# Value matmuls of two key tiles issued together in every second step of an attention loop

## The reference

```python
q = layer_norm(x) @ Wq            # 2048 x 1024, 16 heads of 64
k, v = split(context @ Wkv)       # 1601 keys, and one null key ahead
sim = einsum('bhid,bhjd->bhij', q * sqrt_scale, k * sqrt_scale)
attn = softmax(where(mask, sim, -max))
out = einsum('bhij,bhjd->bhid', attn, v)
out = layer_norm(out @ Wout)
x = x + out
x = x + ffn(layer_norm(x))        # 256 -> 1024 -> 1024 -> 256
```

## Time and profile before

| | us |
|---|---|
| time, median of 3 runs | 1582.44 (1582.07 to 1584.61) |
| span of the profiled execution | 1574.0 |
| time that lies around the span (median less span) | 8.4 |
| PE busy | 1513.6 |
| DVE busy | 1032.6 |
| ACT busy | 708.4 |
| POOL busy | 777.9 |

### The profile page before, as it was taken

The page is one execution under the profiler, slowest core; times in us unless marked ns, Lnnn a source line. Parts: engine busy times, 40 slices in busy tenths (PEclk is TensorE's granted clock), DMA queues, the critical chain, the costliest instruction groups (busy, mean ns, idle before and its releaser), DMA issues.

```text
span 1574.0 us, 20245 instructions
## 1 busy us (share of the span) xinstructions
PE 1513.6 (96%) x6068; PEld 845.3 (54%) x6068; DVE 1032.6 (66%) x1272; ACT 708.4 (45%) x1169; POOL 777.9 (49%) x657
## 2 busy tenths in 40 slices
PE   5898999999999999999999999999999998999998
PEld 3554555455545544554455445554554453778777
DVE  7784677577767766776677567757776747544442
ACT  3324444644464446445544554455445534232242
POOL 3005666576656665666566566656665646101100
PEclk9998999999999999999999999999999999999999
DMA  5222100110020002000200020003000501101000
GB/s 160 79 82 68 51 7 7 34 57 8 12 60 26 7 16 77 7 8 14 77 7 8 15 77 7 11 10 84 8 8 21 178 7 61 61 14 53 13 14 14
DMA packets 43586, 60.22 MB, mean 38 GB/s; under 512 B 4049, under 2 KB 31636, under 8 KB 42580
## 3 DMA queue, kind: packets, MB, share of 16 engines
q1 hardware_dynamic: 43476, 58.92, 12.7%
HBM read 26.27 MB, written 17.30 MB: 28 GB/s over the span
## 4 chain that ended last, share of the span: by engine, by line
PE 89%; DVE 5%; issue 2%; ACT 2%; POOL 1%; DMA 0%; DVEq 0%; SPq 0%; ACTq 0%; POOLq 0%
PE ps_o L1244 25%; PE ps_s L1263 17%; PE ps_s L1264 12%; PE ps_side L1182 12%; PE ps_side L1325 10%; PE ps_side L1168 3%; PE ps_s L1286 3%; PE ps_side L1203 2%; PE ps_side L1158 1%; PE ps_side L1159 1%; DVE mxh L925 1%; PE ps_side L1191 1%; PE ps_o L1142 1%; PE ps_o L1144 1%; DVE khl L914 1%
## 5 line engine op out<-in xcount | busy, mean ns | idle before, releaser
L424 POOL TENSOR_TENSOR acc<-acc,prob 128x512 f32<-128x512 f32 x522 | 669.1, 1299 | 338.5 <-ACT prob L777 311.9
L777 ACT ACTIVATE prob<-ps_s,keybias 128x512 f32<-128x512 f32 x832 | 527.5, 685 | 560.7 <-PE ps_s L1264 518.4
L925 DVE TENSOR_REDUCE mxh<-ps_side 128x1 f32<-128x804 f32 x512 | 485.6, 991 | 152.9 <-PE ps_side L1182 150.3
L1244 PE MATMUL ps_o<-prob,vp 128*64 128x512 f32 x1664 | 448.2, 616 | 0.0
L1263 PE MATMUL ps_s<-qdup,khl 128*128 128x512 f32 x832 | 373.0, 448 | 9.2 <-issue 4.6
L1263 PEld LDWEIGHTS ps_s<-qdup,khl 128*128 128x128 f32 x832 | 156.1, 188 | 365.5 <-issue 261.9
L1264 PE MATMUL ps_s<-qrest,krest 128*128 128x512 f32 x832 | 329.5, 396 | 0.0
L1182 PE MATMUL ps_side<-khl,qdup 128*128 128x402 f32 x1024 | 249.3, 360 | 10.5 <-ACTq L716 4.2
L1182 PEld LDWEIGHTS ps_side<-khl,qdup 128*128 128x128 f32 x1024 | 187.3, 189 | 58.5 <-DVE mxh L925 22.3
L424 DVE TENSOR_TENSOR acc<-acc,prob 128x512 f32<-128x512 f32 x182 | 166.8, 918 | 60.5 <-ACT prob L777 50.2
L1264 PEld LDWEIGHTS ps_s<-qrest,krest 128*128 128x128 f32 x832 | 157.3, 189 | 19.0 <-issue 0.4
(11 more groups left out here) (130 smaller groups left out, 1039.3 us busy)
## 6 DMA issues: line engine op xcount, KB each, us to landing
o_scratch<-onorm SPq DMA_DIRECT2D x32, 256.0 KB, 2.1
otb<-o_scratch SPq DMA_DIRECT2D x4, 2048.0 KB, 8.1
qdup<-qdup SPq DMA_DIRECT2D x14, 512.0 KB, 5.3
v_scratch<-vsb SPq DMA_DIRECT2D x13, 512.0 KB, 3.2
krest<-khl SPq DMA_DIRECT2D x16, 416.0 KB, 5.1
vp<-v_scratch SPq DMA_DIRECT2D x8, 832.0 KB, 7.4
xs<-in_x SPq DMA_DIRECT2D x4, 512.0 KB, 6.8
xres<-in_x SPq DMA_DIRECT2D x1, 2048.0 KB, 11.1
```

Of the source, the lines that this page charges most:

```text
L424: eng.tensor_tensor(a, so_far, prob[g][s % RING][:, :], ALU.add).then_inc(sum_done[g], 1)
L777: act.activation(prob[g][s % RING][:, :], ps_s[g][:, :], ACT.Exp, bias=keybias[:, kt:kt + 1], scale=SCALE).then_inc(p_made[g], 1)
L925: dve.reduce_max(mxh[:, g, qt, half:half + 1], ps_side[slot][:, :, 0:MXW], AX.XY).then_inc(side_free[slot], 1)
L1244: last = pe.matmul(ps_o[qb % 2][hi_rows(g), :], vp[u][:, kt, hi_rows(g)], prob[g][s % RING][:, :], start=(kt == 0), stop=(kt == KT - 1))
```

## The change

In an even step PE issues the value sets of the two steps before, and in an odd one none. In step 0 these are the last two of the pair before; the last pair issues its last two behind step 51. The block sums move to even steps: L from 15, 28, 41 to 16, 28, 42, LP from 7 to 8. The two SA jobs of a step stay two; the SA steps are now 10 to 15, 18 to 27, 30 to 41 and 44 to 47. For head 1 the list of the steps that POOL adds changes: 2, 3, 7, 15 and 41 leave it, 9, 17 and 43 come in. No arithmetic is added or taken away.

```diff
-L_STEPS = {qb: KT * (qb + 1) + 2 for qb in range(QB - 1)}
+L_STEPS = {qb: (KT * (qb + 1) + 3) // 2 * 2 for qb in range(QB - 1)}
...
-LP_STEP = 7
+LP_STEP = 8
...
     if g == 0:
         return True
-    return s % KT in (2, 3) or s in (LP_STEP, LP_STEP + 1) or SA_FIRST <= s <= SA_LAST + 2 and s % 2 == 0
+    l_steps = (LP_STEP, *L_STEPS.values())
+    return s in l_steps or s - 1 in l_steps or SA_FIRST <= s <= SA_LAST + 2 and s % 2 == 0
...
                     for j, job in plan[s]:
                         side(j, job, pair)
-                    if s:
-                        values(n, u, s - 1)
-                    elif not first:
-                        values(n - 1, 1 - u, STEPS - 1)
+                    if s % 2 == 0:
+                        for t in (s - 2, s - 1):
+                            if s:
+                                values(n, u, t)
+                            elif not first:
+                                values(n - 1, 1 - u, STEPS + t)
                     if s == 0:
                         pe.wait_ge(v_loaded, 16 * (n + 1))
                 if last:
+                    values(n, u, STEPS - 2)
                     values(n, u, STEPS - 1)
```

## The result

| | before | after |
|---|---|---|
| time, median, us | 1582.26 | 1597.71 |
| lowest and highest of 4 runs | 1579.28 to 1584.61 | 1597.13 to 1601.30 |
| span of the profiled execution | 1574.0 | 1594.9 |

The ratio is 1.0108, interval 1.0091 to 1.0125: slower, by 15.4 us of the medians and 20.9 us of the two traces. The change put one line into the code ahead of the loop: the score matmuls L1263 and L1264 of before are L1264 and L1265 now, the values L1245, SA L1183, the exponential L778, the reduction L926, the addition L425.

The account below looks back on a forecast made before the run. The time was taken as the sum of what PE (TensorE) issues, unless another engine makes it wait: 95.8 us of new waits against 74.1 saved, +21.7 on 1582.4, gives 1604.1 us, range 1580 to 1628.

Parts of the forecast that it names:

- the two waits: PE in the loop, after odd steps without value sets: waits for exponentials and for reductions, 95.8 us in all.
- saving of a merged pair: Value matmuls of two steps issued together: each merge saves PE 0.33 us, 208 times, 68.6 us.
- wait for D: SA step after odd SA step: PE waits until VectorE reduced the odd step's second SA job; 0.58 us, 77 times.
- wait for the exponentials: After odd steps without a side job, next scores wait for ScalarE to free the score tiles; 0.78 us, 60 times.
- the same behind a block's sum: Exponentials' wait after odd steps 9, 17, 29, 43 and 51 in seven head pairs; 0.78 us each.
- the same behind step 49: Exponentials' wait after step 49, partly covered by a short transpose taken as 0.16; 0.62 us, seven times.
- first query projection's wait: Wait for wq_lo, covered by two value sets in step 0; saves 0.45 us, seven times, 3.2 us.
- The early release: Rival: tiles come free early and PE's restart is hidden, waits total 66.5, less than 74.1 saved; 1575 us, chance 0.12.
- B': Even step's second SA job, forecast to start 2.52 us after the odd step's first SA job, 2.04 unhindered.
- Absent saving: Rival: waits stay but merging saves nothing, as value sets of two key tiles switch the array anyhow; 1673 us, chance 0.02.
- VectorE as the bound: Rival: in SA pairs VectorE's addition waits for both GpSimd additions, 35 us more; 1639 us, chance 0.07.
- The clock: Rival: short gaps in the last head pair bring the 1.2 GHz level, 98 us more; 1702 us, chance 0.03.

Follow-up runs that it names:

- the second job behind the values: Changed kernel, with the second SA job of even two-SA steps issued on PE behind the two value sets instead of ahead; 1557.48 us, ratio to before 0.9867.
- half the reduction: Changed kernel, with VectorE's max reductions over 201 of the 402 columns in each bank; 1550.74 us, ratio to before 0.9816.
- single sets: Changed kernel, with value sets issued singly again where the odd step has no K, Q or SA job; 1576.24 us, ratio to before 0.9982.
- the last experiment: Changed kernel: second SA job behind values, single sets at bare odd steps, VectorE addition between reductions, LP at 6, boundary sets together in step 0; 1538.50 us, 0.9734.

## Why the prediction was right, and where not

**The direction and the two waits.** Slower was forecast with a chance of 0.83, at 1604 us in a range of 1580 to 1628; 1597.7 is inside it. Both waits named are there, at the steps named, and each goes when its cause is taken away (the second job behind the values; half the reduction; single sets).

**The sum, term by term.** Forecast +21.7, the traces +20.9. That these two are so close is in part luck: the misses in the table have both signs, and the trace of before was a short one (see the base, below).

| term | forecast | measured |
|---|---|---|
| saving of a merged pair | 0.33 | 0.31 (SA, halved reduction), 0.35 (queries, 7.01 to 6.66) |
| value run of eight records | 1.87 | 1.87 |
| wait for D, a pair of steps | 0.58, 77 times | 0.56, 77 times |
| wait for the exponentials, last head pair | 0.78, 25 times | 0.68 (4.62 less 3.94, which is 4.27 - 0.33) |
| the same behind a block's sum | 0.78, 35 times | 0.77 (step 17: 1.59 for 1.04; step 18: 3.84 for 3.62) |
| the same behind step 49 | 0.62, 7 times | 0.59 (step 49: 1.59 for 1.20; step 50: 3.11 for 2.91) |
| first query projection's wait, gone | 0.45, 7 times | 0.64 (step 1: 3.06 with one set in step 0, 2.42 with two), 6 times |
| second SA job of step 10 waits for LP's tile | not seen | 0.69, 6 times |
| head pair inside the loop | +1.5 | +1.8 (151.2 to 153.0) |
| last head pair, its first 51 steps | +10.9 | +9.1 (131.0 to 140.1), 0.9 of it for the set that its step 0 took over from the pair before |

Two sizes and two counts of the working were off, and one wait was missed. The counts: the last head pair's last two sets stood together before already, behind step 51, so there were 207 merges and not 208; and the first head pair has no value set in its step 0, so its wait for wq_lo stayed (1.1 us before, 1.0 after), and 0.45 was saved six times and not seven. The sizes: the restart after an ACT end was taken as 0.10 from the earlier trace rows, where PE waited for the increment that ScalarE issues behind the copy; behind an exponential itself it is 0.05. In the last head pair the exponentials also started at 0.78 (1257.36 less 1256.58) and not at 0.85; why isn't known. The wait that was missed: the sentence that L at 8, 16 and 42 only "comes a step later" looked at who reads the normalised block and not at who needs the tile of the sum: behind LP only one step lies before SA begins, and VectorE's 3.36 us hold it. The experiment with LP at step 6 shows that term alone. It cost 4.1 us, which the smaller waits of the last head pair (25 x 0.10 = 2.5) and the larger saving ahead of the queries (6 x 0.64 for 7 x 0.45, 0.7 more) gave back in good part.

**The base was wrong by 6 us.** The sum was made against the profiled execution, and then 8.4 us were said to lie outside the span and to stay. Each execution's time is now known beside its own span: the difference is 1.7 to 2.2 us in nearly all (2.8 once), in every kernel. The profiled execution of before was one of the short ones: 20 others beside the experiments had spans of 1573.7 to 1580.7. With 2.1 the same working gives 1574.0 + 2.1 + 21.7 = 1597.8, and the measured median is 1597.7. That is closer than the method allows: it sets a short execution of before against the middle of after. By medians the change is +15.4, or +18.6 against the 20 others (1579.1), and not +21.7.

No experiment tried what makes executions of one kernel differ by some 7 us, but the records point at the granted clock; that it is the cause isn't shown. Of the 20, the 12 whose mean granted clock was 0.992 or more had a median span of 1576.2, the 8 at 0.991 or less 1579.8. Some traces show places. One is the loop's back edge: PE's waits there add up to 4.1 to 6.9 us in them, and in some the clock then stands at the 1.2 GHz level for a while. In the last experiment's trace, behind a wait of 3.45, the score matmuls of step 0 start 0.43 apart instead of 0.23 (PE, and the window 568 to 572, columns as in the earlier trace rows):

```profile
568.00 0.79 PE L1268 MATMUL ps_s<-qdup,khl 128*128 128x512 f32 x1 [3.45 <-issue]
...
569.01 0.63 PE L1268 MATMUL ps_s<-qdup,khl 128*128 128x512 f32 x1
569.44 0.63 PE L1269 MATMUL ps_s<-qrest,krest 128*128 128x512 f32 x1
...
568.00:572.00 4.00, 4.00 (x8) 2.51 (x8) 0.00 (x0) 1.38 (x2) 0.00 (x0) 0.50 0.03 10
```

The traces of the kernel before and of the changed one have no such place at the back edge: their granted clock behind both crossings is 1.00, after waits of 2.1 to 2.5 us.

**The rivals.** The early release (1575) would have needed B' at 2.44 behind C; the start is at 2.52. Absent saving: the value run is 1.87. VectorE as the bound would have given SA pairs of 6.4; they take 5.99. Its addition did collide (median 1561 ns, before 685) and came after one GpSimd addition, not two, ending 4.1 behind C as worked out:

```profile
L425 DVE TENSOR_TENSOR acc<-acc,prob x196: 658/1561/1775, 145.1 to 1347.9; 128x512 f32<-128x512 f32 x196
```

The clock: through the loop it stayed at 1.00, the 2.4 GHz level, in spite of a short wait in nearly every pair of steps, and so it did in the last head pair but for one place. Windows of the changed kernel, columns as in the earlier trace rows:

```profile
300.00:1200.00 900.00, 859.28 (x3528) 455.96 (x3525) 706.47 (x676) 435.45 (x712) 546.89 (x426) 1.00 0.10 28
1210.00:1260.00 50.00, 46.70 (x176) 19.04 (x178) 34.92 (x25) 27.18 (x44) 27.82 (x20) 1.00 0.45 155
1326.00:1332.00 6.00, 4.17 (x11) 1.32 (x11) 5.75 (x6) 1.95 (x3) 1.50 (x2) 0.72 0.00 0
```

The last row is step 44 of the last head pair. There VectorE is busy for 5.6 us with the first block's tail (L1020), its addition comes late, the second head's exponential waits 2.6 us for it and PE for the exponential. Behind that wait the granted clock fell, and eight value records took 2.97 us (1328.98 to 1331.95) where they take 1.87 elsewhere:

```profile
1327.84 0.79 PE L1264 MATMUL ps_s<-qdup,khl 128*128 128x512 f32 x1 [2.59 <-ACT prob L778]
...
1328.98 3.04 PE L1245 MATMUL ps_o<-prob,vp 128*64 128x512 f32 x8
1331.95 0.50 PE L1264 MATMUL ps_s<-qdup,khl 128*128 128x512 f32 x1
```

So the clock did drop, but in one step and not for the whole head pair. It cost about 1.6 us: 1.10 in the values, and 0.48 in the two score matmuls ahead (1327.84 to 1328.98 is 1.14, where it is 0.66 in step 22: 1258.68 to 1259.34). The sum had neither this wait nor this drop. They don't show in the +9.1 of the last head pair, because the kernel before had waits of its own in steps 40 to 46, which come to about as much (an estimate: 20.7 us for these seven steps, of which 15.8 are seven sideless steps and a sum; after the change 22.2, of which 17.8).

The Trainium skill ("TensorE: Matmul & The Clock Gate", A second HAM failure mode: psum-queue depth-cycling) lets short idling between groups bring the clock down; with waits of 0.3 to 0.7 us every 5 to 6 us and PE busy for 93 to 95% that didn't happen here. It happened behind single waits of over 2 us, and not behind all of them.

## What to carry to other kernels

A value set between two users of a tile with one or two buffers is not only work, it is the cover of a wait: before merging two of them, write down for each tile with one or two buffers when its reader ends, and what PE has left to issue until then. Here the merge was worth 0.33 us a pair and uncovered 0.56 to 0.77; with one job moved behind the merged run, and no merge where the odd step has nothing else to issue, the same idea is 2.6% faster than before instead of 1% slower. Look also at the places outside the regular steps (the first head pair, the last block's sum, the back edge, the tail's work on VectorE): that is where the counts and the waits of this forecast were off. And take the base of a forecast from the time of the execution whose trace is read, or say that it isn't known.

## What the runs showed that was not expected

- A wait in the list of PE's idle time is shorter than the delay it causes: 77 waits of 20.7 us in all, 0.27 each, cost 0.56 each. Part of the wait lies under the tail of the matmul before, and the first matmuls behind it start 0.10 late.
- The collision of the additions is a matter of phase: in the changed kernel VectorE's take 1561 ns at the median, with one PE job moved 692 ns, with the same two engines doing the same additions.
- Behind some waits of PE of over 2 us the granted clock went to the 1.2 GHz level for a few us (2.6 us in step 44, 3.45 us at the back edge); behind others (2.5 us at the back edge of the changed kernel) it did not.
- A 128x402 job put between value sets and score matmuls instead of before both takes 0.03 us more a pair (5.46 against 5.43 with the halved reduction).
